# The first item of a fused Mamba and convolution kernel: its setup laid out anew

## The reference

```python
def _mamba(x, W_in, conv_w, conv_b, W_x, W_dt, b_dt, A_log, D_skip, W_out):
    xc, z = split(einsum('bld,ed->ble', x, W_in))
    xc = silu(causal_depthwise_conv4(xc, conv_w) + conv_b)
    dbc = einsum('ble,re->blr', xc, W_x)
    dt = softplus(dbc[..., :8] @ W_dt.T + b_dt)
    Bm, Cm, A = dbc[..., 8:24], dbc[..., 24:], -exp(A_log)
    h[t] = exp(dt[t] * A) * h[t - 1] + (dt[t] * xc[t]) * Bm[t]      # 256 channels x 16 states
    y = (einsum('bdn,bn->bd', h, Cm) + xc * D_skip) * silu(z)
    return einsum('ble,de->bld', y, W_out)
y1 = _mamba(x, *weights1) + _mamba(x, *weights2) + x
# then: relu(batch_norm(y1)) -> conv3x3(mean|w0| * sign(w0)) -> relu(batch_norm) -> conv3x3(mean|w1| * sign(w1)) -> + y1
```

## Time and profile before

| | us |
|---|---|
| median of three runs | 839.22 (838.72 to 839.31) |
| time of the profiled execution | 841.76 |
| its span, first to last instruction | 840.0 |
| busy in the span: PE, VectorE, ScalarE, GpSimd | 757.2, 746.6, 732.9, 708.5 |
| mean granted clock of PE | 0.98 |

### The profile page before, as it was taken

One profiled execution on the slowest core, in us unless ns is written; L12 is line 12 of the kernel. 1 busy time (PEld: TensorE's weight loads), 2 busy tenths in 40 slices (PEclk: granted clock), 3 DMA queues, 4 the chain that ended last, 5 costly groups with the idle time before them and its releaser, 6 DMA issues.

```text
span 840.0 us, 13183 instructions
## 1 busy us (share of the span) xinstructions
PE 757.2 (90%) x4542; PEld 383.9 (46%) x4542; DVE 746.6 (89%) x479; ACT 732.9 (87%) x1319; POOL 708.5 (84%) x334
## 2 busy tenths in 40 slices
PE   8788989898998989898999999899989897898998
PEld 4534334343544443434343434444444434547876
DVE  2798999999999999999999999999999999895141
ACT  4789999999999999999999999999999999875050
POOL 0658999999999999999999999999999999890000
PEclk9699999999999999999999999999999999999999
DMA  7807062444425151717071715343352616100011
GB/s 204 301 4 266 36 224 81 171 159 133 172 85 219 67 214 45 258 54 276 26 254 50 251 54 210 120 165 140 113 192 75 226 52 232 51 1 1 1 38 62
DMA packets 39146, 110.97 MB, mean 132 GB/s; under 512 B 7244, under 2 KB 9384, under 8 KB 39080
## 3 DMA queue, kind: packets, MB, share of 16 engines
q1 hardware_dynamic: 37724, 109.84, 37.4%
q10 hardware_dynamic: 1356, 0.29, 0.2%
HBM read 106.97 MB, written 3.15 MB: 131 GB/s over the span
## 4 chain that ended last, share of the span: by engine, by line
DVE 53%; issue 24%; PE 11%; ACT 6%; POOL 3%; SPq 2%; DMA 1%; DVEq 0%; ACTq 0%; POOLq 0%
DVE state L915 25%; DVE bank L915 22%; PE bank L1334 8%; DVE state L925 3%; POOL state L610 2%; ACT product L729 2%; ACT bank L698 1%; ACT state L709 1%; SPq L418 1%; DVE k_room L937 1%; PE bank L1122 1%; DMA k_room<-in_L_conv_w_dram 1%; PE bank L1056 1%; DVE x_tok L937 1%; POOL state L601 1%
## 5 line engine op out<-in xcount | busy, mean ns | idle before, releaser
L610 POOL TENSOR_TENSOR state<-state,wide 128x1024 f32<-128x1024 f32 x164 | 384.8, 2368 | 11.0 <-DVE state L915 11.0
L601 POOL TENSOR_TENSOR state<-u,wide 128x1024 f32<-128x1024 f32 x124 | 292.2, 2371 | 8.8 <-PE bank L1122 8.8
L1122 PE MATMUL bank<-state,ident 64*64 64x512 f32 x2048 | 254.5, 606 | 1.2 <-POOL state L610 1.2
L915 DVE TENSOR_TENSOR_SCAN state<-state,bank 128x1024 f32<-128x1024 f32 x100 | 225.7, 2271 | 1.9 <-PE bank L1115 1.9
L729 ACT ACTIVATE product<-u_tok,b_tok 128x256 f32<-128x256 f32 x528 | 219.0, 496 | 0.8 <-PE bank L1115 0.3
L1115 PE MATMUL bank<-ident,product 128*128 128x128 f32 x1056 | 144.4, 281 | 62.8 <-ACT product L729 32.8
L1115 PEld LDWEIGHTS bank<-ident,product 128*128 128x128 f32 x1056 | 116.0, 143 | 158.7 <-issue 84.9
L698 ACT ACTIVATE bank<-dt,a_neg 128x512 f32<-128x512 f32 x248 | 160.2, 677 | 22.4 <-DVE state L915 16.0
L709 ACT ACTIVATE state<-dt,a_neg 128x512 f32<-128x512 f32 x264 | 171.5, 711 | 0.0
L915 DVE TENSOR_TENSOR_SCAN state<-bank,state 128x1024 f32<-128x1024 f32 x64 | 145.3, 2271 | 1.8 <-ACT bank L698 1.8
L915 DVE TENSOR_TENSOR_SCAN bank<-bank,state 128x1024 f32<-128x1024 f32 x60 | 137.1, 2284 | 3.7 <-ACT bank L698 2.8
(11 more groups left out here) (102 smaller groups left out, 507.2 us busy)
## 6 DMA issues: line engine op xcount, KB each, us to landing
wide<-bc_rows SPq DMA_DIRECT2D x176, 512.0 KB, 6.6
wide<-bc_rows SPq DMA_DIRECT2D x32, 256.0 KB, 3.6
x_t<-in_x_dram SPq DMA_DIRECT2D x4, 512.0 KB, 4.9
out_dram<-x_t SPq DMA_DIRECT2D x8, 256.0 KB, 2.0
k_room<-in_L_conv_w_dram SPq DMA_DIRECT2D x2, 576.0 KB, 4.5
bc_rows<-dbc SPq DMA_DIRECT2D x16, 64.0 KB, 1.6
state<-in_L_conv_W_in_dram SPq DMA_DIRECT2D x2, 256.0 KB, 3.6
x_tok<-in_x_dram ACTq DMA_DIRECT2D x1, 256.0 KB, 3.7
```

Source lines behind the costliest of these rows:

```text
L601: pool.tensor_tensor(tile(n), u[:, :, :], over_halves(b_wide[:, PLAIN.index(s), :]), ALU.mult).then_inc(plain_input, 1)
L610: pool.tensor_tensor(tile(n), tile(n), over_halves(c_wide[:, n % NST, :]), ALU.mult).then_inc(output_pool, 1)
L915: dve.tensor_tensor_scan(flat(target), flat(decay), flat(source), 0.0, ALU.mult, ALU.add).then_inc(scanned, 1)
L1122: return pe.matmul(y_sum[64 * h:64 * h + 64, b, :], weights[rows, :], source[rows, h, :], start=first, stop=last)
```

## The change

SP issues the kernels' loads ahead of the large load of x, and W_out of both Mambas last. The groups have a new order (x of item 2's chunk at 7, W_dt of Mamba 1 at 10, both W_out at 14 and 15, the rest of x from 16), and groups 10 to 15 share banks in separate columns (`SHARED`), so that PE can fill them one after the other; a group waits only for a copy whose columns meet its own. The turned u and B of item 0 go to banks 2, 3 and 6 instead of one bank in turn. PE runs the W_out groups just ahead of turning the input of state 1. VectorE sums the magnitudes ahead of u, copies group 8, and then makes the input of state 0 itself; its copies of groups 9 to 21 stand behind the scans of states 0 to 3. ScalarE turns the rates of Mamba 0 ahead of the first xc, takes the signs between the two halves of xc, drops one table load, gets B after both halves of u, and begins with the products of state 1 before its decays; it takes over the skip diagonal of Mamba 1. PE projects the first half of item 1's taps between two x groups of slot 0. The kernels are transposed and copied one at a time, in slots 8 and 9 of items 1, 2 and 3.

```diff
-AT_KERNELS = (8, 9, 10)
+AT_KERNELS = (1, 2, 3)
+PE_KERNELS = 8
+ACT_KERNELS = 9
+ACT_RATES = 2
+ACT_THIRD = 2
+ACT_DIAGONAL = 3
...
+        GROUPS = [x_group(0), *tap_groups(0), z_group(0), *small_groups(0), x_group(1), *tap_groups(1),
+                  small_groups(1)[2], z_group(1), *small_groups(1)[:2], out_group(0), out_group(1), *(x_group(g) for g in range(2, TOKENS // CHUNK))]
...
-        BY_ACT = (0, 2, 17, 19, 21)
+        BY_ACT = (0, 2)
+        GROUPS_FIRST, GROUPS_AT_TAPS, GROUPS_AT_DBC = range(0, 4), range(4, 7), range(7, 8)
+        GROUPS_AT_B_TOK, GROUPS_AT_U_TOK, GROUPS_AHEAD = range(8, 11), range(11, 14), range(14, 16)
+        GROUPS_INSIDE = (range(16, 18), range(18, 20), range(20, NG))
+        COPIES_INSIDE = (range(9, 16), range(16, 18), range(18, 20), range(20, NG))
...
+        SHARED = {10: (6, 256), 11: (7, 0), 12: (7, 256), 13: (7, 264), 14: (4, 0), 15: (4, 256)}
+        ALONGSIDE = {11: 13, 12: 13, 14: 15}
...
@@ block.sync @@
             load_w_in(sp, 1)
             load_conv_w(sp, 1)
+            for n in range(2):
+                sp.dma_start(k_raw[n], t[f"L1_conv_w{n}"].rearrange("o i a b -> o (i a b)")).then_inc(load_k, 16)
             load_x_tokens(sp, 2)
-            load_w_out(sp, 0)
             load_w_x(sp, 1)
             load_vectors(sp, 1)
             load_w_dt(sp, 1)
             load_a_log(sp, 1)
+            load_w_out(sp, 0)
             load_w_out(sp, 1)
...
@@ gpsimd times_b @@
+                if n == 0:
+                    return
                 wait(pool, u_ready, k + 1)
+                if n == PLAIN[1]:
+                    pool.wait_ge(plain_input, 1)
...
@@ scalar prepare @@
                         if k == 0 and h == 0:
                             gates(0)
+                            act.wait_ge(load_k, K_LOADS)
+                            for n in range(2):
+                                act.activation(k_sign[n], k_raw[n], ACT.Sign).then_inc(k_signed, 1)
...
                 if s == ACT_DT:
-                    act.preload_act_table_set("softplus")
+                    if k > 0:
+                        act.preload_act_table_set("softplus")
...
-                        a_log(0)
                         plain_decays(0)
-                        a_log(1)
...
             for g in BY_ACT:
-                if g < GROUPS_AT_DT[0]:
-                    setup_copy(act, copy, g, setup_act)
+                setup_copy(act, copy, g, setup_act)
+            a_log(0)
...
+                    if k == 0 and s == ACT_RATES:
+                        a_log(1)
+                    if k == 0 and s == ACT_DIAGONAL:
+                        skip_diagonal()
+                    if k < 0 and s == NST - 1:
+                        turned_decays(TURNED[0])
+                        plain_decays(PLAIN[1])
+                        products(TURNED[1])
+                    if k == 0 and s == ACT_THIRD:
+                        products(TURNED[2])
...
+                    if k in AT_KERNELS and s == ACT_KERNELS:
+                        kernels(k)
...
@@ vector @@
+            def first_input():
+
+                dve.wait_ge(b_loaded[0], 16)
+                dve.wait_ge(u_ready, 1)
+                dve.tensor_tensor(tile(0), u[:, :, :], over_halves(b_wide[:, 0, :]), ALU.mult).then_inc(plain_input, 1)
...
-            skip_diagonal(0)
+            skip_diagonal()
             scale_taps(1)
-            copies(GROUPS_AT_DBC)
             magnitudes(0)
             magnitudes(1)
+            copies(GROUPS_AT_DBC)
             first_u()
-            copies(GROUPS_AT_DT)
-            skip_diagonal(1)
-            copies(GROUPS_AT_B_TOK)
+            copies(GROUPS_AT_B_TOK[:1])
+            first_input()
...
                     if k >= 0:
                         times_c(n)
+                    if k == 0 and s < len(COPIES_INSIDE):
+                        copies(COPIES_INSIDE[s])
...
@@ tensor, the loop @@
+                    if k < 0 and s == NST - 1:
+                        for g in GROUPS_AHEAD:
+                            transposes(g)
...
-                    if k == 0 and s < 2:
-                        for g in GROUPS_INSIDE[s]:
+                    if k == 0 and s == 0:
+                        for g in GROUPS_INSIDE[0]:
+                            transposes(g)
+                        for part in range(KCONV):
+                            project(1, part)
+                        for g in GROUPS_INSIDE[1]:
+                            transposes(g)
+                    if k == 0 and s == 1:
+                        for g in GROUPS_INSIDE[2]:
                             transposes(g)
...
+                    if k in AT_KERNELS and s == PE_KERNELS:
+                        kernels(k)
```

More of the change, by code:

```diff
@@ L874, in copies @@
                 for g in groups:
+                    if g == 10:
+                        dve.wait_ge(b_tok_ready, 1)
                     if g not in BY_ACT:
@@ L1040, in transposes @@
                 what, which, sources, cols, _, _ = GROUPS[g]
-                there = [q for q in range(g) if setup_place(q) == setup_place(g)]
+                there = [q for q in range(g) if meet(q, g)]
                 if there:
```

135 lines of the change are left out of this document (71 added, 64 removed).

## The result

| | before | changed | ratio, 95% interval |
|---|---|---|---|
| time, median (lowest to highest), us | 839.26 (838.72 to 840.99) | 833.21 (831.75 to 833.65) | 0.9926 (0.9905 to 0.9947) |
| profiled execution: time, span | 841.76, 840.0 | 833.54, 831.7 | |
| first scan of item 0, of item 1, of item 15, last scan | 33.06, 87.43, 709.35, 750.86 | 26.05, 76.83, 701.13, 742.65 | |

The change made the kernel 6.05 us faster, not 10.1; 833.2 is just above the range's end of 833.0. By the interval of the ratio the gain lies between 4.4 and 8.0 us, so the kernel is faster, to which the prediction gave 0.93. Between the two profiled executions the difference is 8.2 us.

A forecast was written before the change was run, and what follows sets the result against it. VectorE, GpSimd and ScalarE were taken as full at once, with GpSimd carrying the loop from item 1's product of state 23. Lead 10.7 less 0.6 given back is 10.1, so 839.2 - 10.1 = 829.1 us; range 826.9 to 833.0.

The forecast's parts named there:

- Steps 1 and 2: Kernel start to first scan of item 0: u starts at 22.1, scan 0 at 26.4 for 33.06, lead 6.7.
- Step 3: Item 0, scan 0 to scan 4: some 15.5 us, 0.2 for PE's half clock; scan 4 at 42.1, lead 5.2.
- Step 4: Item 0, scan 4 to GpSimd's u of item 1: 20.0 us for 22.36, lead +2.4.
- step 5: To GpSimd's product of state 23: its idle 1.86 and 1.24 go, +3.1, total 10.7; VectorE's bound 11.0.
- step 6: Given back: kernel copies on ScalarE in items 1 to 3, 0.2; z projection at half clock on PE, 0.4.
- Rival (c): ScalarE loses the kernel copies' full cost in items 1 to 3, 2.8; gain 7.5, time 831.7; chance 0.08.
- Step 7: SP's DMA queue: hold ends near 14, issues through at 19.3 for dbc; between +0.5 and -3, taken as 0.
- (d): Slower: W_out of Mamba 1, last in SP's queue, lands late; gain gone after 39, 843 at 43; chance 0.04.
- (e): Item 0: copies again wait for PE's transposes of x (5.6), ScalarE still holds up scans; 839; chance 0.03.
- (b): SP's queue late: hold ends at 16, dbc store at 21.4, B 2 to 3 later; gain 7.6, 831.6; chance 0.12.
- (a): PE bounds item 0, half clock in both places, 0.8 and 1.1 more; gain 8.2, time 831.0; chance 0.14.

The follow-up runs named there:

- warm_first: Changed kernel plus 5, 8 and 14 transposes that nobody reads on PE where it waited in item 0; 831.43 us, ratio 0.9888.
- kernels_item0: Changed kernel with the convolution kernels' transposes and copies back in slots 8 to 10 of item 0, signs still early; 832.66 us, ratio 0.9919.
- add_one_later: Changed kernel with VectorE's addition of item 15's output one slot later, behind state 5 instead of 4; 831.41 us, ratio 0.9903.
- no_kernel_copies: Changed kernel without the convolution kernels' PE transposes and ScalarE copies, constants in their place, so convolutions are not computed; 829.74 us, ratio 0.9884.
- loads_last: Changed kernel with the convolution kernels' loads last in SP's list again and the signs in slot 7 of item 0; 835.71 us, ratio 0.9938.
- gpsimd_extra: Changed kernel with some 1.1 us of small memsets added on GpSimd in slot 7 of item 6; 833.41 us, ratio 0.9928.
- vector_extra: Changed kernel with one unused VectorE sum over 128 x 1024, about 1.2 us, added in item 6; 833.74 us, ratio 0.9939.
- before_again: The kernel before, unchanged, run once more as a kernel of its own for a second profile; 839.89 us, ratio 1.0003.
- first_by_pool: Changed kernel with the input of state 0 of item 0 made by GpSimd again instead of VectorE; 832.84 us, ratio 0.9929.

## Why the prediction was off, step by step

**Steps 1 and 2 held.** The first scan came at 26.05 (26.4 forecast). The rates' load landed at 9.0, not 8.0, and ScalarE waited 0.82 for it; of the 1.3 us to spare that left enough, and xc was held by VectorE, not by this:

```profile
9.03 0.23 ACT L701 ACTIVATE a_neg<-a_neg 128x32 f32<-128x32 f32 x1 [0.82 <-DMA a_neg<-in_L_conv_A_log_dram]
...
11.86 0.69 ACT L790 ACTIVATE xc<-bank,vectors 128x512 f32<-128x512 f32 x1 [0.95 <-DVE vectors L522]
14.39 2.21 ACT L795 ACTIVATE k_room<-k_room 128x1152 bf16<-128x1152 f32 x2
17.34 0.69 ACT L790 ACTIVATE xc<-bank,vectors 128x512 f32<-128x512 f32 x1 [0.74 <-PE bank L1163]
```

The second xc is at 17.34 for 16.72, so u came at 22.79, not 22.1. The 0.6 arises at the very start of the kernel: PE's first ten weight transposes take 1.99 us for 1.25 before, and its taps start at 7.73 for 7.12 (the changed kernel's row, then that of before):

```profile
5.80 1.99 PE L1114 MATMUL bank<-ident,state 128*128 128x128 f32 x10
```

```profile
5.64 1.25 PE L1056 MATMUL bank<-ident,state 128*128 128x128 f32 x10
```

It is not of the change either. In the changed kernel the first six of the ten took 0.42 us each and the last 0.27; in before, in warm_first and in kernels_item0 all ten took 0.27. In the half clock of item 15 (granted 0.50) PE's 128x128 matmuls also take 0.42, so PE most likely still ran at 1.2 GHz there. The profile's granted clock reads full at that place, so this rests on the durations alone. u starts between 21.9 and 22.8 in the kernels with the changed setup, and it starts early in those with short transposes (21.97 in kernels_item0).

B had landed by 24.79, a little earlier than forecast. The signs fit their gap. The rates' load landed 1 us later than the 8.0 assumed, but no run shows that the kernels' loads are the cause: it landed between 8.05 (add_one_later) and 10.72 (no_kernel_copies) beside them, and at 8.24 in loads_last, which moves them to the end of the queue. The rule of the Trainium skill that each DMA engine takes turns between queues by packets (DMA: Bandwidth & Descriptors, Queues, rings and completion order) is neither borne out nor refuted by this. The 1.3 us to spare were used up by 10.01 in gpsimd_extra, whose xc started at 11.91 with no wait but the one for the rates ahead of it.

**Step 3 nearly held**: state 4 at 42.38, forecast 42.1, with one wait of 1.35 us for PE. Its cause, half clock, was named; its price was 1.0, taken with 0.2. From the first scan it is 16.33 us for the 15.7 of the sum; the first scan was 0.35 ahead of the sum and so hid part of it. warm_first, without half clock there, took 14.70.

**Step 4 was short by 0.9.** GpSimd's u of item 1 started at 63.30, 20.9 behind the scan of state 4 (20.0 forecast, 22.36 before): a lead of 6.4 for the 7.6 of steps 3 and 4. It cost nothing, because GpSimd is not the bound (step 5). GpSimd waited in item 0 where the sum had none:

```profile
51.01 2.35 POOL L637 TENSOR_TENSOR state<-u,wide 128x1024 f32<-128x1024 f32 x1 [4.99 <-PE bank L1184]
55.34 2.35 POOL L646 TENSOR_TENSOR state<-state,wide 128x1024 f32<-128x1024 f32 x1 [1.97 <-DVE state L973]
```

**Step 5 named the wrong engine, and its number was right by luck.** VectorE's lead at item 1 was 10.6, where the step had 11.0 for VectorE. The 10.7 that it used was GpSimd's, for the product of state 23, and this came 9.6 earlier (100.57 for 110.15):

```profile
100.57 2.40 POOL L646 TENSOR_TENSOR state<-state,wide 128x1024 f32<-128x1024 f32 x1
```

"It carries the loop from there on", read off 49.77 busy of 50, is wrong: GpSimd's u of item 2 came 9.5 us earlier (107.78 for 117.31), less than VectorE's lead, and that cost VectorE nothing; run gpsimd_extra made GpSimd 1.07 later without effect, and run vector_extra passed on 0.97 of 1.20. The kernel before shows it too: GpSimd's u came every 44.45 us (117.31, 161.76, 206.20) while VectorE took 44.24 for items 2 and 3, so GpSimd fell back 0.2 an item and held up nobody. An engine without idle time may be ahead of all who need its results. The two bounds were close here, so this fault cost 0.1 us in the sum; it also led step 6 astray.

**Step 6 failed.** For the copies in items 1 to 3 it took 0.2 of a range of 0 to 3.1, because "VectorE is a little faster than GpSimd". The measured loss is 1.7. With VectorE as the one that carries the loop there is no such cover: each copy delays the decays for the next scan. ScalarE in item 1, without a gap from the copy to the late decays:

```profile
108.41 1.00 ACT L689 ACTIVATE k_t<-bank 128x1024 bf16<-128x1024 bf16 x1
109.31 1.28 ACT L737 ACTIVATE bank<-dt,a_neg 128x512 f32<-128x512 f32 x2
...
118.61 1.71 ACT L768 ACTIVATE product<-u_tok,b_tok 128x256 f32<-128x256 f32 x4
120.23 1.28 ACT L737 ACTIVATE bank<-dt,a_neg 128x512 f32<-128x512 f32 x2
```

The loss is 0.46 + 0.90 + 0.34 = 1.7 against before, and run no_kernel_copies gives it all back. Rival (c) had the mechanism, with 2.8 as its price, and its sign, VectorE waiting for ScalarE in items 1 to 3, is there. So is the prediction's own sign for such a fault, a first scan at 26 and a gain of less than 7, which pointed behind scan 4, to step 4 or 6. The other term of the step, 0.4 for a z projection at half clock, has no wait of VectorE that answers to it.

**Step 7 held.** The issue queue was held from 5.76 to 12.51 (14 forecast) and was through at 17.3, ahead of dbc; the store of dbc went at 19.96, because dbc itself was 0.65 later. Rivals (d) and (e) did not come about. The sign of (b), a store after 19.8, is there, but not its cause: the queue was free. The sign of (a) is there as well, 1.2 GHz from 31.2 to 34.6 us with VectorE waiting 1.35 for PE; by warm_first's item 0 it is worth about 1.6, though PE did not become the bound of item 0.

**The carrying over failed as well, and its cause is in part open.** Of the 10.1 the profiled executions kept 8.2: 1.5 went in items 1 to 3 (1.7 for 0.2), 0.6 in items 9 and 13, 0.1 in item 4, and 0.1 of the lead, while the 0.4 of step 6 did not occur. Of the medians' 10.1, 6.05 came. The last 2.2 lie between profile and median: the profiled execution of before was 2.5 above its median, that of the changed kernel 0.3. The sum took the profile's time and subtracted the same amount from the median; that supposes the two executions are alike. Item 15 took 41.5 in that profile of before and 40.0 in the next, while the changed kernel took 41.5 in both of its profiles. If most executions of before have the short item 15 and most of the changed kernel the long one, this is 1.5 of the 2.2. That is not shown: how often each occurs with either kernel was not measured, and the second profile of before was still 1.1 above its median with the short item. The mean clock does not settle it. In the changed kernel a lower mean goes with the shorter time (0.984 to 0.986 took 833.5 to 833.9, 0.982 took 832.9, 0.971 to 0.979 took 831.5 to 832.3), but in the twelve executions of before_again it does not (0.965 to 0.971 took 837.9 to 841.5, 0.980 to 0.982 took 839.0 to 841.0). The first profile of before, at 841.76, was also one of the slowest of its kernel: in all later jobs its executions took 837.8 to 841.9.

**Open:** the holes of 0.3 us in items 9 and 13, 0.6 in all, which no step had. They come back at the same instruction in both profiles of the changed kernel and in most variants, and are in neither profile of before; no_kernel_copies has only that in 13, vector_extra and first_by_pool lack that in 13, and first_by_pool has one in item 8. No run singled out their cause.

## What to carry to other kernels

Idle time tells which engines are not the bound, but not which of several full ones is: add one operation of known length to each and see whose period grows. Work that moves from the first item to later ones is not hidden merely because another engine is as busy; count it wherever its engine's results are needed in time for the next step of the engine that carries the loop. And before a profiled difference is carried over to medians, compare two profiles of the same kernel: where they differ by more than the term in question, that difference belongs in the range.

## What the runs showed of the hardware

- The same program has 1.5 us more or less in one item, by where a stretch of PE at 1.2 GHz falls (41.5 for item 15 in 6 profiles with one some 9 us into it, 40.0 in 7 without, none of them with an edit there).
- Transposes that nobody reads, put where PE stood idle, kept it at 2.4 GHz from 27 to 66 us and took item 0 from 50.8 to 49.2 us; with such transposes in item 15 the half clock came at 701.3 instead of 710.4, but it came at 701.1 and 701.3 in kernels_item0 and vector_extra without them.
- The first scan of kernels with the same setup lies anywhere from 25.4 to 26.4 us; u, 3 us ahead of it, is early where PE's first ten transposes take 1.25 us and late where they take 1.99.
- SP's issue of one load of W_x took 6.75 us (5.76 to 12.51) while the large loads ahead of it ran, and the three behind it 0.25 to 0.32 each.
